# Graph attention's second half: the inverse in two parts and the kept sums added in units of their own, with a filler of products moved into the gap after the stage

## The reference, cut to what matters

```python
z = _layernorm(x, ln_att_g, ln_att_b)
q, k, v = (z @ Wq.T + bq), (z @ Wk.T + bk), (z @ Wv.T + bv)      # each reshaped to (n, H, D)
s = jnp.einsum('ehd,ehd->eh', q[src], k[dst]) / np.sqrt(D) + att_bias
p = jnp.exp(s - m[src])
denom = jax.ops.segment_sum(p, src, num_segments=n)
alpha = p / jnp.where(denom[src] == 0, 1.0, denom[src])
agg = jax.ops.segment_sum(alpha[:, :, None] * v[dst], src, num_segments=n)
x = x + agg.reshape(n, C) @ Wo.T + bo
z = _layernorm(x, ln_ff_g, ln_ff_b)
return x + jax.nn.silu(z @ W1.T + b1) @ W2.T + b2
```

## Time and profile before

| | |
|---|---|
| median of 3 runs | 2241.63 us (2235.17 to 2244.38) |
| profiled execution | 2240.67 us, its span 2238.0 us, mean granted clock 0.975 |
| TensorE busy over the span | 2054.4 us (92%) |
| VectorE, ScalarE, GpSimd busy | 1334.1, 749.9, 705.8 us |
| chain that ended last | TensorE 49%, DMA 16%, GpSimd 14%, VectorE 11%, issue 5% |
| second half of attention | from about 826 to 998.8 us of the span |

### The profile page before, as it was taken

The page is one execution under the profiler, slowest core; times in us unless marked ns, Lnnn a source line. Parts: engine busy times, 40 slices in busy tenths (PEclk is TensorE's granted clock), DMA queues, the critical chain, the costliest instruction groups (busy, mean ns, idle before and its releaser), DMA issues.

```text
span 2238.0 us, 30116 instructions
## 1 busy us (share of the span) xinstructions
PE 2054.4 (92%) x11364; PEld 1239.4 (55%) x11364; DVE 1334.1 (60%) x3184; ACT 749.9 (34%) x1498; POOL 705.8 (32%) x500
## 2 busy tenths in 40 slices
PE   4998987999999979989999999999999999999977
PEld 2556555543346545547764467678666644455554
DVE  6666567888999977651224543441222243289997
ACT  4211122331038753412223355654111111134553
POOL 1346878888775535430000000000000000024442
PEclk9998988999999999999999999999999999999989
DMA  9995232223349976652000010004000023000000
GB/s 318 388 373 142 3 78 3 21 22 31 50 78 233 228 203 173 177 153 87 1 10 0 1 77 1 1 1 187 2 1 0 1 58 97 0 1 10 10 15 14
DMA packets 122049, 181.89 MB, mean 81 GB/s; under 512 B 67761, under 2 KB 69451, under 8 KB 118071
## 3 DMA queue, kind: packets, MB, share of 16 engines
q1 hardware_dynamic: 76833, 178.51, 25.2%
q0 software_dynamic: 45072, 1.46, 5.6%
HBM read 109.21 MB, written 70.71 MB: 80 GB/s over the span
## 4 chain that ended last, share of the span: by engine, by line
PE 49%; DMA 16%; POOL 14%; DVE 11%; issue 5%; ACT 3%; SPq 1%; DVEq 0%; PEldq 0%; ACTq 0%; POOLq 0%; PEld 0%
DMA edge_table<-arena 15%; POOL edge_table L627 14%; PE banks L204 12%; PE banks L2586 6%; PE banks L2537 6%; PE banks L1868 3%; PE banks L2345 2%; PE banks L2333 2%; PE banks L2320 2%; PE banks L2970 2%; PE banks L2369 2%; PE banks L1664 2%; PE banks L1685 1%; DVE arena L1554 1%; PE banks L198 1%
## 5 line engine op out<-in xcount | busy, mean ns | idle before, releaser
L627 POOL DMA_INDIRECT edge_table<-arena x313 | 519.2, 1659 | 263.8 <-DMA edge_table<-arena 159.8
L204 PE MATMUL banks<-arena 128*125 128x512 f32 x1200 | 551.2, 606 | 15.5 <-DVE arena L3190 14.3
L204 PEld LDWEIGHTS banks<-arena 128*125 128x125 f32 x1200 | 219.9, 191 | 259.0 <-issue 241.8
L2997 POOL CAST arena<-arena 125x128 f32<-125x128 uint32 x10 | 2.9, 290 | 692.1 <-DVE arena L3133 692.0
L1554 DVE TENSOR_TENSOR arena<-banks,arena 125x1000 f32<-125x1000 f32 x100 | 180.8, 1822 | 27.6 <-ACT banks L1638 27.2
L2476 DVE SCALAR_TENSOR_TENSOR arena<-banks,arena 125x512 f32<-125x512 f32 x80 | 60.1, 751 | 170.1 <-PE banks L2586 170.1
L2212 DVE CUSTOM_DVE_ANT_0 arena<-banks,arena 125x512 f32<-125x512 f32 (+8 forms) x144 | 73.0, 553 | 128.8 <-PE banks L2320 126.0
L2586 PE MATMUL banks<-arena 128*125 128x512 f32 x320 | 144.5, 595 | 0.0
L2537 PE MATMUL banks<-arena 128*128 128x250 f32 x640 | 141.6, 374 | 0.1
L1664 PE MATMUL banks<-arena 64*125 64x250 f32 x800 | 113.9, 404 | 29.3 <-DVE arena L1554 28.8
L2537 PEld LDWEIGHTS banks<-arena 128*128 128x128 f32 x640 | 120.5, 189 | 28.4 <-issue 15.7
(11 more groups left out here) (385 smaller groups left out, 3443.3 us busy)
## 6 DMA issues: line engine op xcount, KB each, us to landing
edge_table<-arena SPq DMA_DIRECT2D x23, 2304.0 KB, 21.3
arena<-edge_table SPq DMA_DIRECT2D x100, 326.8 KB
arena<-edge_table SPq DMA_DIRECT2D x50, 330.8 KB
arena<-L_ffn_W SPq DMA_DIRECT2D x4, 2048.0 KB, 10.0
adjacency<-arena SPq DMA_DIRECT2D x50, 109.4 KB
arena<-adjacency SPq DMA_DIRECT2D x10, 546.9 KB
edge_table<-arena POOLq DMA_INDIRECT x313
arena<-edge_table SPq DMA_DIRECT2D x100, 37.9 KB
```

The lines of the kernel that those rows point to most:

```text
L204: last = nc.tensor.matmul(dst, xT[:, i, :], w[:, i, 0:n], start=(i == 0), stop=(i == k - 1))
L627: pool.indirect_dma_start(d["table"], bass.IndirectOffsetOnAxis(ap=cell[0:EP, c:c + 1].bitcast(U32), axis=0), vals[0:EP, c * ROW:(c + 1) * ...
```

## The change

In a late pass VectorE's extra work is dealt out anew. The inverse starts behind the weighting of r = 4 and not 3, without its clamp, and its reciprocal is split by columns: 125 of them there, the other 125 behind r = 5. The kept values are added behind r = 3 and r = 6, and the multiplications alone stand behind r = 7 and r = 8. TensorE spreads the inverses at r = 5 and 7 and not at 4 and 6. In an early pass the copy becomes a maximum with 1e-37, also behind r = 4. At the stage's end TensorE waits for the three feed-forward weight loads ahead of the barrier, and the six unused products stand right behind the barrier, ahead of the wait for the other loads.

```diff
-        DEN, SPREAD, OUT = 2, (4, 6), (8, 0)
+        DEN, SPREAD, OUT = 2, (5, 7), (8, 0)
+        INVERSE_AT, VALUES_AT, DIVIDE_AT = (4, 5), (3, 6), (7, 8)
...
                 if not late:
-                    nc.vector.tensor_copy(kept, now).then_inc(a_r, 1)
+                    nc.vector.tensor_scalar(kept, now, 1e-37, None, ALU.max).then_inc(a_r, 1)
                     return
                 link(dve, nc.vector.tensor_tensor(rden, now, kept, ALU.add))
-                link(dve, nc.vector.tensor_scalar(rden, rden, 1e-37, None, ALU.max))
-                nc.vector.reciprocal(rden, rden).then_inc(a_r, 1)
+                nc.vector.reciprocal(rden[:, 0:TP], rden[:, 0:TP])
+
+            def rest_of_inverse():
+                nc.vector.reciprocal(rden[:, TP:CHUNK], rden[:, TP:CHUNK]).then_inc(a_r, 1)
+
+            def divided_part(c, half):
+                return qT_g[:, 2 * half:2 * half + 2, sources(c)]
+
+            def add_values(c, half):
+                dve.wait_ge(a_raw, CHUNKS + c + 1)
+                part = divided_part(c, half)
+                link(dve, nc.vector.tensor_tensor(part, part, values_kept[:, c, 2 * half:2 * half + 2, :], ALU.add))
 
             def divide(c, half):
-                dve.wait_ge(a_raw, CHUNKS + c + 1)
-                part = qT_g[:, 2 * half:2 * half + 2, sources(c)]
-                link(dve, nc.vector.tensor_tensor(part, part, values_kept[:, c, 2 * half:2 * half + 2, :], ALU.add))
+                part = divided_part(c, half)
                 dve.wait_ge(a_bc, 2 * c + half + 1)
...
                 if g >= 1:
-                    if r == DEN + 1:
+                    if r == INVERSE_AT[0]:
                         inverse(g - 1)
                     if g > CHUNKS:
+                        if r == INVERSE_AT[1]:
+                            rest_of_inverse()
                         for half in range(2):
-                            if r == SPREAD[half] + 1:
+                            if r == VALUES_AT[half]:
+                                add_values(g - CHUNKS - 1, half)
+                            if r == DIVIDE_AT[half]:
                                 divide(g - CHUNKS - 1, half)
...
             inverse(PASSES - 1)
+            rest_of_inverse()
             for half in range(2):
+                add_values(CHUNKS - 1, half)
                 divide(CHUNKS - 1, half)
...
+            pe.wait_ge(s_wf, 16 * 3)
             leave_stage(pe, "PE")
+            unused_products(bank(4), w2_g[:, 0, :], 6)
...
-            unused_products(bank(7), w2_g[:, 0, :], 6)
             turn(0)
```

## The result

| | before | after |
|---|---|---|
| median of 5 runs, us | 2239.94 (2235.17 to 2244.38) | 2218.39 (2214.95 to 2222.98) |
| profiled execution, its span | 2240.67, 2238.0 | 2218.39, 2216.6 |
| mean granted clock | 0.975 | 0.979 |
| TensorE, VectorE busy | 2054.4, 1334.1 | 2043.5, 1329.7 |

The ratio is 0.991, with a 95% interval of 0.989 to 0.993. The forecast was 2216.

A forecast was written before the change was run, and what follows sets the result against it. TensorE was taken as the bound of the late passes, with holes waiting for VectorE. Gains of 15.5 + 3.1 (last pass) + 0.2 + 6.0 = 24.8 us off 2240.67 gave 2215.9, forecast 2216, range 2209 to 2227.

The forecast's parts named there:

- The passes: Late attention passes under the new order: 34.31 us of TensorE work plus 0.15 of stalls, 34.5 us each.
- The two stalls of 0.08 and 0.07 at W5 and W7: TensorE's scores would wait 0.08 and 0.07 us for VectorE's weightings of r = 5 and r = 7.
- The step on the value addition: Late passes: an addition of kept values beside GpSimd is slowed to 1.15 us from 0.62, not blocked.
- The half reciprocal: Reciprocal of 125 columns on VectorE in late passes, taken as 0.94 us, with bounds of 0.86 and 1.72.
- Rival C: Value additions blocked by GpSimd's running instruction, 2.5 us each; some 3.7 us a pass, 15 in all: 2231; chance 0.06.
- Rival B: VectorE stays the bound at r = 5 and 7, half reciprocals 1.7 us each beside GpSimd; 2222 to 2224; chance 0.25.
- Passes 6 to 8: Three late attention passes together: 118.85 us before less 103.4 after, a gain of 15.5 us.
- The clock term: Passes 6 to 8: 6.2 of the 15.5 us gain from products at 1.2 GHz behind the 2.3 us wait.
- The border: Attention to feed-forward: six products start at the barrier, first transposes move from 1010.1 to 1004.1, gain 6.0 us.
- The tail: Attention's end: clamp alone 0.3 us, not 0.57 beside GpSimd; the split gives 0.1 back; gain 0.2 us.
- rival D: Slower: without holes TensorE gets 1.2 GHz for long; gain gone at 25 us, 2266 at 50; chance 0.04.
- Nothing for the early passes: Early passes save about 0.5 us each, but the table wait takes it; otherwise worth some 2.4 us more.

The follow-up runs named there:

- the delay alone: Kernel before, with the whole inverse (clamp kept) and the spreads one unit later in late passes; 2232.21 us, ratio 0.9986.
- the loop alone: Changed kernel with the old border: wait for all seven loads, then the barrier, then the six unused products; 2227.21 us, ratio 0.9939.
- later-load kernel: Changed kernel with the load of the first three quarters of `w1` issued six blocks later, in pass 7; 2220.57 us, ratio 0.9906.

## Why the prediction came true, point by point

**The passes.** Forecast 34.5, measured 34.49 and 34.50 in passes 7 and 8, though the parts differ. The two stalls of 0.08 and 0.07 at W5 and W7 don't exist, since the value addition is 0.67 and not 1.15 long and the chain arrives early. In their place the spread costs more once it stands alone: 1.05 us (946.89 to 947.93 and 952.85 to 953.89, from its start to that of TensorE's next work, scores in the first case and values in the second) against the 0.95 I had taken from 960.34 to 961.28.

**The step on the value addition failed.** "The trace doesn't bear it out" rested on splitting GpSimd's pair of 5.02 us in the middle. A narrower window of the same trace parts the pair, and has VectorE's clamp of the same pass beside the GpSimd instruction ahead of it:

```profile
951.76 2.31 POOL L1591 TENSOR_TENSOR arena<-arena 125x1000 f32<-125x1000 f32 x1 [3.52 <-DVE arena L1554]
953.72 0.50 DVE L1521 TENSOR_SCALAR arena<-arena 128x250 f32<-128x250 f32 x1
957.79 2.32 POOL L1591 TENSOR_TENSOR arena<-arena 125x1000 f32<-125x1000 f32 x1 [3.73 <-DVE arena L1554]
960.06 2.75 POOL L1591 TENSOR_TENSOR arena<-arena 125x1000 f32<-125x1000 f32 x1
```

The first of the pair had ended at 960.11, and the second, held up, took 2.75. The addition of 959.49 to 960.64 had stood until 960.11 and run 0.53: blocked, not slowed. The clamp says the same: it ended at 954.22, 0.15 behind GpSimd's end at 954.07, as it did behind the 874.47 of the delay alone. Rival C's mechanism is true, with 2.17 us for one addition and one clamp. Its price didn't fall due, since in the new order the addition is released by the same weighting as GpSimd and is first. The term of 1.15 was mis-sized by 0.48. That C stayed away has another reason than the one I gave: the order of the change happened to put both additions ahead of GpSimd, and that was luck. With the first addition behind r = 5 it costs 35.71 less 34.50 = 1.2 us a pass.

**The half reciprocal** is 0.94, as the line through 128x250 and 125x10 gave. Rival B needed 1.7 of it; GpSimd beside it costs it nothing.

**Passes 6 to 8: 14.04 against 15.5.** The miss is pass 6. I had put late blocks beside `w1` at up to 1 us in the range; they cost 1.25 here, and in kernels close to this one up to 2.67 of wait and a low clock with it.

**The clock term.** 6.2 of the 15.5 us were one execution's. The other profiled executions with the same loop had 1.6 and none. Against passes of 37.56 us at the full clock the loop is worth 3.06 us in each of four passes, 12.2 in all, and the loop alone measured 13.3 by its medians. The sum came out against the trace because it was made against the execution that had that low clock. Against the medians it can't tell: without the 6.2 it would have been 18.6 us, about as near the measured 21.55 as the recorded 24.8.

**The border** gave 6.08 against 6.0, the products 5.42 against 5.2, at the full clock. In four further executions with the old border it took 12.3 to 13.0 us, so the gain is 6.1 to 6.7. **The tail** gave 0.30 against 0.2.

**Two slips in the working.** In rival D the stretch from 826 to 1004 is 178 us and not 150. A pass like the last is 34.3 of work and 3.24 of waits, not 34.1 and 3.4; the sum of 37.5 is right. Neither moves the forecast.

**Nothing for the early passes:** as forecast. TensorE's wait for the table grew from 9.13 to 13.54 us, and the first late scores behind it came at 818.62 where they had come at 818.82. Most of that growth isn't the change's: attention's first scores came 3.80 us earlier in this execution (643.53 against 647.33). From there to the denominators at r = 2 of pass 5 the changed kernel takes 147.65 us, the kernel before 148.55, so the early passes gained 0.9 here and not 2.4.

**Not forecast:** the stages behind took 1.4 us more. The change doesn't touch their work. Over the 150 us from 1010 the granted clock was 1.00 before, 0.99 after and 0.97 in the later-load kernel, and the time from the transposes to the end lies between 1227.9 and 1235.4 us over all profiled executions here. What lowers the clock there stays open.

## What to carry to other kernels

When one engine's extra work stalls another through a ring of buffers, put each piece a step behind its inputs' arrival and ask first which piece can be left out: here a clamp of 250 columns kept 1.95 us of wait in each pass, and the splitting was worth at most 0.17. A short VectorE operation between SBUF tensors must be released together with or ahead of GpSimd's next long one; read the two instructions of a merged row one by one, in a narrower window, before you split it in your head. A loss of clock seen in one execution isn't a term of the sum until a second one shows it.

## What the runs showed of the hardware that was not expected

- VectorE's addition of 128x500 and its clamp of 128x250, both from SBUF to SBUF, stood until GpSimd's running instruction of 2.31 us was over (2.17 us each), then took 0.53 and 0.15. Half reciprocals, and additions that read PSUM, kept their times beside the same GpSimd instructions (0.94 and 0.40).
- Waits of 2.3 to 2.4 us in the four late passes 6 to 9 of the same kernel were followed by 1.2 GHz in three of them in one execution and in one in another; in the one execution with the same loop and the new border in none. In the kernel with the delay alone a wait of 1.94 to 1.97 us was followed by it in three of the four. What decides it stays open.
- The table gate moves by itself. GpSimd's last scatter was issued at 805.47 us in one execution of the kernel before and at 795.71 in another, and the first late scores behind the denominators of pass 6 at 834.28 and 826.35. Both are executions of one kernel, so a difference of two spans can hold these 8 us; the lengths of passes don't.
